# Row sums of the attention: an adding DMA puts the second key tile's probabilities into the first, and the probabilities are laid out by query tiles, then heads

## The chip, the cores and the metric

The kernel runs on one core of a Trainium2 chip: TensorE (PE, with a separate track for weight loads), VectorE (DVE), ScalarE (ACT), GpSimd (POOL), SyncE (SP, which here only issues DMAs), an SBUF of 128 partitions, eight PSUM banks and 16 DMA engines. The metric is the device time of one execution in microseconds (us).

## What is computed

One transformer layer on x of 4 x 512 rows of 1024: causal attention with 32 query heads and 8 key/value heads of 32, residual and layer norm, then a gated feed-forward with ternary weights, residual and layer norm.

```python
q = _apply_rope(q, cos, sin); k = _apply_rope(k, cos, sin)
k = jnp.repeat(k, N_REP, axis=2); v = jnp.repeat(v, N_REP, axis=2)
scores = jnp.einsum('bqhd,bkhd->bhqk', q, k) / np.float32(np.sqrt(HEAD_DIM))
scores = scores + mask
attn = jax.nn.softmax(scores, axis=-1)
out = jnp.einsum('bhqk,bkhd->bqhd', attn, v).reshape(bsz, seq_len, -1) @ wo
x = _layernorm(x + out)
x = _layernorm(x + (silu(x @ gate_w.T) * (x @ up_w.T)) @ down_w.T)
```

## The kernel before

**Stages.** The first 70 us load and project, the attention lasts until about 735 us, the feed-forward takes the rest. The attention runs over 16 units (u: a batch and eight query heads), each of two groups (G: four query heads that share one key/value head). That makes 32 groups, q = 2u + G; this text counts them from one, so the 15th group is u = 7, G = 0.

**A group.** Its 512 keys are four tiles of 128, taken in the order j = 3, 2, 1, 0. Key tile j is seen only by the queries from 128 j on, so its probabilities are a tile `p32[j]` of 128 keys (partitions) by four heads by 512 - 128 j queries, in f32. For each tile PE makes scores by keys (`score_k`, L984), ACT takes the exponential into `p32[j]` (`exp`, L1139), POOL zeroes the causal triangle of the diagonal block (`causal`, a select, L1443), and PE multiplies with v (`pv`, L998) into bank 7, all four tiles accumulating.

**Row sums.** The sum over keys of each query is a product with a matrix of ones (`sums`, L1013) into bank 2. So that it need not run over four tiles, POOL adds tiles first (`presum`, L1451): tile 3 into the fitting columns of tile 2 after the product of tile 2, then tile 2 into tile 1 after the product of tile 1. The sum runs over two tiles, 512 and 384 columns; in the very last group, where nothing is presummed, over four. DVE then transposes the sums, takes reciprocals, transposes back and scales bank 7 (`sum_turn`, `att_scale`, L1291 to L1301). Only when this is done may the next group's first product write bank 7. The scaled rows are split into two f16 parts (`att_hi`, `att_lo`) and stored; the output projections of a batch (`proj out`, on L948 with `wo_parts`) read them back when all eight groups of that batch are stored.

**Reuse.** There is one set of `p32`. The exponential of a group's tile j waits for what last read that tile in the group before: its product, and the sum (tiles 0 and 1) or a presum (tiles 2 and 3).

**Other work in the same stage.** PE also runs the projections of later units (`proj q`, 24 matmuls of 256 columns per tile; `proj kv` and `proj out`, 512 columns), and scores by queries (`score_q`, L960, with a mask product L963) two units ahead, whose row maxima DVE takes (`row_max`, L1267). They are the filler between the dependent steps above.

**What sets the order.** A planner (`Plan`) gives every piece of work an engine, a rank, a duration, the pieces it must follow and a time until its result is seen elsewhere. It plays these through and writes down one fixed order per engine. The programs then issue their instructions in that order, each with its semaphore waits. An engine that waits holds up all that stands behind it.

## Time and profile before

| | us |
|---|---|
| median of 2 runs | 1869.38 (1867.28 to 1871.48) |
| the profiled execution's own time | 1868.12 |
| its span, first to last instruction | 1866.4 |
| PE busy | 1807.0 (97%) |
| DVE busy | 1187.7 (64%) |
| ACT busy | 710.5 (38%) |
| POOL busy | 543.6 (29%) |

Busy time is what the instructions of an engine cover, so overlapping matmuls count once. An engine's idle time is named after what ended it (its releaser). A row of the trace's timeline merges instructions that follow each other on one line, and its duration runs to the modelled end of the last one; matmuls overlap, so the time that a piece takes on PE is read from its start to the start of the next row.

### The profile page before, as it was taken

What the parts mean: (1) busy time and instruction counts of PE and PEld (TensorE: products, weight loads), DVE (VectorE), ACT (ScalarE), POOL (GpSimd) and SP (SyncE); (2) the same over time, 40 slices, a digit from 0 to 9 for tenths busy, and PEclk for the clock granted to TensorE, in tenths of its full rate; (3) what the DMA queues carried; (4) which work ended last, traced back from release to release, by engine and by line L of the source; (5) the groups of instructions that cost most, each with busy time, mean ns of one, the idle gap of its engine ahead of it and who ended that gap; (6) DMA issues with size and microseconds to landing.
All of it is one profiled execution on the core that took longest, in us unless ns stands there. A gap on an engine that the chain in (4) does not pass through costs nothing.

```text
span 1866.4 us, 27364 instructions
## 1 busy us (share of the span) xinstructions
PE 1807.0 (97%) x10528; PEld 882.0 (47%) x10528; DVE 1187.7 (64%) x2047; ACT 710.5 (38%) x1112; POOL 543.6 (29%) x845
## 2 busy tenths in 40 slices
PE   7889999999999998999999999999999999999997
PEld 4545655555555543444444444444444444444443
DVE  7877778668768764445544444745656765667645
ACT  5443444444434444436433343342232322222221
POOL 1354546456546564131000000211321211112103
PEclk9999999999999999999999999999999999999999
DMA  8543234334334398557644353649321211232301
GB/s 246 118 103 78 54 85 125 83 80 116 90 52 114 81 212 221 209 208 263 236 171 150 107 195 126 215 148 211 127 66 53 79 66 51 72 104 85 107 12 79
DMA packets 228162, 233.13 MB, mean 125 GB/s; under 512 B 183872, under 2 KB 184128, under 8 KB 228032
## 3 DMA queue, kind: packets, MB, share of 16 engines
q1 hardware_dynamic: 227168, 230.99, 42.2%
q8 instruction: 83, 1.36, 0.3%
q10 hardware_dynamic: 864, 0.39, 0.1%
q14 instruction: 47, 0.39, 0.1%
HBM read 122.55 MB, written 72.88 MB: 105 GB/s over the span
## 4 chain that ended last, share of the span: by engine, by line
PE 85%; DVE 6%; issue 3%; SPq 2%; POOL 2%; ACT 1%; DMA 1%; ACTq 0%; DVEq 0%; POOLq 0%
PE bank L1053 31%; PE bank L948 20%; PE bank L1074 13%; PE bank L1087 6%; PE bank L998 4%; PE bank L960 3%; PE bank L984 3%; PE bank L1013 2%; SPq L1587 2%; DVE down_forms L1391 1%; PE bank L963 1%; DVE gate_blocks L1385 1%; POOL p_tiles L1451 1%; DVE row_max L1267 0%; DVE up_blocks L1375 0%
## 5 line engine op out<-in xcount | busy, mean ns | idle before, releaser
L1053 PE MATMUL bank<-x_forms,weight_forms 128*128 128x512 f16 x3136 | 700.9, 379 | 12.7 <-DVE gate_blocks L1375 4.4
L1053 PEld LDWEIGHTS bank<-x_forms,weight_forms 128*128 128x128 f16 x3136 | 305.3, 98 | 387.0 <-DVE gate_blocks L1375 7.1
L1139 ACT ACTIVATE p_tiles<-bank 128x512 f32<-128x512 f32 (+1 forms) x352 | 193.0, 556 | 276.6 <-PE bank L984 273.5
L1267 DVE TENSOR_REDUCE row_max<-bank 128x1 f32<-128x384 f32 (+3 forms) x352 | 220.0, 636 | 98.2 <-PE bank L963 96.6
L1074 PE MATMUL bank<-down_forms 128*128 128x512 f16 x1152 | 259.6, 381 | 2.4 <-issue 2.4
L948 PE MATMUL bank<-wq_parts,xT_parts 128*128 128x256 f16 x1536 | 219.4, 275 | 8.9 <-DVE wq_parts L1231 8.7
L1410 DVE TENSOR_TENSOR acc<-bank,acc 128x512 f32<-128x512 f32 x188 | 127.6, 687 | 124.2 <-PE bank L1074 64.7
L1443 POOL TENSOR_SCALAR_AFFINE_SELECT p_tiles<-p_tiles 128x128 f32<-128x128 f32 (+2 forms) x352 | 139.0, 403 | 212.2 <-ACT p_tiles L1139 210.9
L1074 PEld LDWEIGHTS bank<-down_forms 128*128 128x128 f16 x1152 | 113.0, 98 | 139.7 <-issue 4.9
L948 PEld LDWEIGHTS bank<-wq_parts,xT_parts 128*128 128x128 f16 x1536 | 144.1, 98 | 56.8 <-issue 14.2
L948 PE MATMUL bank<-wo_parts,att_parts 128*128 128x512 f16 x672 | 170.1, 382 | 0.6 <-DMA att_parts<-att_spill 0.6
L1475 POOL TENSOR_TENSOR acc<-acc,down_forms 128x1024 f32<-128x1024 f32 x16 | 38.8, 2427 | 377.4 <-DVE acc L1410 377.4
L1087 PE MATMUL bank<-down_forms 128*128 128x512 f16 x560 | 133.6, 379 | 1.7 <-DVE down_forms L1391 1.7
L960 PE MATMUL bank<-k_stack,q_stack 96*128 96x512 f16 (+3 forms) x512 | 127.0, 303 | 5.1 <-DVE row_max L1267 5.1
L984 PE MATMUL bank<-q_stack,k_stack 98*128 98x384 f16 (+3 forms) x512 | 126.4, 301 | 4.6 <-ACT p_tiles L1139 3.1
L1451 POOL TENSOR_TENSOR p_tiles<-p_tiles 128x512 f32<-128x512 f32 (+1 forms) x62 | 115.8, 1868 | 49.4 <-PE bank L998 41.3
L1375 DVE TENSOR_TENSOR up_blocks<-bank,up_blocks 128x512 f32<-128x512 f32 x84 | 57.9, 690 | 112.9 <-PE bank L1053 59.6
L1214 ACT ACTIVATE down_forms<-gate_blocks 128x512 f16<-128x512 f32 x102 | 64.0, 628 | 136.4 <-DVE gate_blocks L1385 130.4
L998 PE MATMUL bank<-p_tiles,v 128*32 128x128 f32 (+3 forms) x1024 | 95.4, 453 | 11.6 <-POOL p_tiles L1443 10.4
L1375 DVE TENSOR_TENSOR gate_blocks<-bank,gate_blocks 128x512 f32<-128x512 f32 x84 | 57.8, 688 | 74.8 <-PE bank L1053 65.0
L948 PE MATMUL bank<-wkv_parts,xT_parts 128*128 128x512 f16 x384 | 98.3, 379 | 1.3 <-DVE wkv_parts L1231 1.3
L1458 POOL TENSOR_SCALAR rstd<-rstd 128x1 f32<-128x1 f32 x96 | 34.8, 363 | 220.2 <-DVE rstd L1329 213.8
(114 smaller groups left out, 1999.9 us busy)
## 6 DMA issues: line engine op xcount, KB each, us to landing
weight_forms_spill<-weight_forms SPq DMA_DIRECT2D x28, 896.0 KB, 5.7
weight_forms<-weight_forms_spill SPq DMA_DIRECT2D x28, 896.0 KB, 4.5
x_forms_spill<-x_parts SPq DMA_DIRECT2D x56, 256.0 KB, 2.4
w_page<-gateT SPq DMA_DIRECT2D x28, 512.0 KB, 5.0
w_page<-upT SPq DMA_DIRECT2D x28, 512.0 KB, 4.0
w_page<-downT SPq DMA_DIRECT2D x28, 512.0 KB, 4.3
att_spill<-att_made SPq DMA_DIRECT2D x64, 128.0 KB, 2.1
down_forms<-x_spill SPq DMA_DIRECT2D x16, 512.0 KB, 3.4
```

Of the source, the lines that this page charges most:

```text
L948: t = nc.tensor.matmul(dst, left[:, a, k, rows], right[:, c, k, cols], start=k == 0 and m == 0, stop=last)
L960: nc.tensor.matmul(to[:, h, :], qT[0:STK, u % QS, h0 + h, i * P:n], kT[0:STK, b % 2, kv_of(u, h0 + h), 0:n], start=h == 0, stop=False, ski ...
L984: t = nc.tensor.matmul(to[:, h, :], kT[0:STKM, b % 2, (u % UNITS) * UG + G, lo:lo + P], qT[0:STKM, u % QS, G * REP + h0 + h, lo:S], start= ...
L998: t = nc.tensor.matmul(bank[PV_BANK[q]][h * HD:(h + 1) * HD, lo:S], value, p32[j][:, h, :], start=j == NT - 1, stop=j == 0, tile_position= ...
L1053: t = nc.tensor.matmul(strassen[bank_set(use)][to][:, :], w_form[:, use % 4, A_FORMS[a_form], k * P:(k + 1) * P], xF[:, :, B_FORMS[b_form] ...
L1074: t = nc.tensor.matmul(to[:, :], hid_p[place_of(r)][:, k, a, i // 2 * P:(i // 2 + 1) * P], wd_p[place_of(r)][:, c, cols], start=r == round ...
L1087: t = nc.tensor.matmul(to[:, :], hid_f[r % NF % 3][:, HID_FORMS.index(a_form), a, pair * P:(pair + 1) * P], wd_f[r % NF % 3][:, DOWN_B[b_f ...
L1139: nc.scalar.activation(p32[j][:, h0:h0 + heads, :], bank[5 + m % 2][:, 0:heads * n].rearrange("p (h c) -> p h c", c=n), ACT.Exp, scale=SCO ...
L1267: nc.vector.tensor_reduce(mx[:, u % 2, i, h0:h0 + ROW_HEADS[i]], bank[3 + m % 2][:, 0:ROW_HEADS[i] * n].rearrange("p (h c) -> p h c", c=n) ...
L1410: nc.vector.tensor_tensor(dst, got[:, :], dst, ALU.add).then_inc(s_acc, 1)
L1443: nc.gpsimd.affine_select(out=block, in_=block, compare_op=ALU.is_ge, fill=0.0, base=0, pattern=[[0, KEY_HEADS[j]], [1, P]], channel_multi ...
L1451: nc.gpsimd.tensor_tensor(to, to, p32[j + 1][:, :, :], ALU.add).then_inc(s_pre, 1)
```

## The change

For the first 29 groups (`EARLY`) a DMA that adds, issued by POOL, puts `p32[1]` (which by then holds tiles 1 to 3) into the columns of `p32[0]` from 128 on, 768 KB, and the row sum runs over `p32[0]` alone. The last three groups are summed as before. So that both sides of the DMA are one run of 1536 numbers in each partition, `p32[j]` is laid out by query tiles, then heads, then queries in a tile, where it was heads, then queries. The sum waits for the DMA; the exponential of the next group's tile 1 waits for the DMA where it waited for the sum. The planner takes the DMA's issue at 1.2 us and its landing at 5.0 us and ranks these sums 3.5 us later; it then writes another order for the whole attention.

```diff
+EARLY = NU * UG - 3
+FOLD_ISSUE, FOLD_LANDS = 1.2, 5.0
+
+def summed(q):
+    return 1 if q < EARLY else 2 if q < NU * UG - 1 else NT
...
-        freed = [("pv", *last, j), ("sums", *last) if j < 2 else ("presum", *last, j - 1)] if q else []
+        freed = [("pv", *last, j), ("sums", *last) if j < summed(q - 1) else ("presum", *last, j - 1) if j > 1 else ("fold", *last)] if q else []
...
-        put(PE, at + 3.5, 3.0 if final else 1.5, "sums", u, G, takes="T", after=[("causal", *one)] + [("presum", u, G, 1)] * (not final))
+        if q < EARLY:
+            put(PO, at + 3.5, FOLD_ISSUE, "fold", u, G, after=[("pv", u, G, 0), ("presum", u, G, 1)], lands=FOLD_LANDS)
+        put(PE, at + (7 if q < EARLY else 3.5), (.9, 1.6, 2.2, 2.5)[summed(q) - 1], "sums", u, G, takes="T", after=[("causal", *one)] + (
+            [("fold", u, G)] if q < EARLY else [("presum", u, G, 1)] if not final else []))
...
-        p32 = [p_all[:, p_starts[j]:p_starts[j + 1]].rearrange("p (h c) -> p h c", h=REP) for j in range(NT)]
+        p32 = [p_all[:, p_starts[j]:p_starts[j + 1]].rearrange("p (i h c) -> p i h c", h=REP, c=P) for j in range(NT)]
...
-                        t = nc.tensor.matmul(bank[PV_BANK[q]][h * HD:(h + 1) * HD, lo:S], value, p32[j][:, h, :],
+                        t = nc.tensor.matmul(bank[PV_BANK[q]][h * HD:(h + 1) * HD, lo:S], value, p32[j][:, :, h, :],
...
-                    tiles = 2
-                    if u * UG + G == NU * UG - 1:
-                        tiles = NT
-                    else:
-                        on.wait_ge(s_pre, 2 * (u * UG + G + 1))
+                    q = u * UG + G
+                    tiles = summed(q)
+                    if tiles == 1:
+                        on.wait_ge(s_fold, 16 * (q + 1))
+                    elif tiles == 2:
+                        on.wait_ge(s_pre, 2 * (q + 1))
...
-                    nc.scalar.activation(p32[j][:, h0:h0 + heads, :], bank[5 + m % 2][:, 0:heads * n].rearrange(
-                        "p (h c) -> p h c", c=n), ACT.Exp, scale=SCORE_DOWN).then_inc(s_exp, 1)
+                    nc.scalar.activation(p32[j][:, :, h0:h0 + heads, :], bank[5 + m % 2][:, 0:heads * n].rearrange(
+                        "p (h i c) -> p i h c", h=heads, c=P), ACT.Exp, scale=SCORE_DOWN).then_inc(s_exp, 1)
...
-                    block = p32[j][:, h0:h0 + KEY_HEADS[j], 0:P]
+                    block = p32[j][:, 0, h0:h0 + KEY_HEADS[j], :]
...
-                    to = p32[j][:, :, P:S - j * P]
-                    nc.gpsimd.tensor_tensor(to, to, p32[j + 1][:, :, :], ALU.add).then_inc(s_pre, 1)
+                    to, more = (t.rearrange("p i h c -> p (i h c)") for t in (p32[j][:, 1:NT - j, :, :], p32[j + 1][:, :, :, :]))
+                    nc.gpsimd.tensor_tensor(to, to, more, ALU.add).then_inc(s_pre, 1)
+                elif kind == "fold":
+                    u, G = which
+                    q = u * UG + G
+                    on.wait_ge(s_pv, NT * (q + 1))
+                    on.wait_ge(s_pre, 2 * (q + 1))
+                    to, more = (t.rearrange("p i h c -> p (i h c)") for t in (p32[0][:, 1:NT, :, :], p32[1][:, :, :, :]))
+                    e.dma_start(to, more, accum_op=ALU.add).then_inc(s_fold, 16)
```

**Place one: PE at the end of the 15th group.** In the rows below `p_tiles,v` is a product with v, `p_tiles,ones` the row sum, `k_stack,q_stack` and `cmask,idB` a score by queries with its mask, `q_stack,k_stack` a score by keys, `wo_parts` and `wq_parts` projections. Before, from the group's last product on:

```order
L998 MATMUL bank<-p_tiles,v 32x512 x4
L1013 MATMUL bank<-p_tiles,ones 32x512 x4
L1013 MATMUL bank<-p_tiles,ones 32x384 x4
L948 MATMUL bank<-wo_parts,att_parts 128x512 x3
L984 MATMUL bank<-q_stack,k_stack 128x256 x2
L960 MATMUL bank<-k_stack,q_stack 128x512
L963 MATMUL bank<-cmask,idB 128x128
L948 MATMUL bank<-wo_parts,att_parts 128x512 x3
L984 MATMUL bank<-q_stack,k_stack 128x256 x2
L948 MATMUL bank<-wo_parts,att_parts 128x512 x3
L998 MATMUL bank<-p_tiles,v 32x128 x4
```

Now, from the same product on (line numbers are those of the changed kernel):

```order
L1013 MATMUL bank<-p_tiles,v 32x512 x4
L999 MATMUL bank<-q_stack,k_stack 128x256 x2
L975 MATMUL bank<-k_stack,q_stack 128x512
L978 MATMUL bank<-cmask,idB 128x128
L963 MATMUL bank<-wo_parts,att_parts 128x512 x3
L999 MATMUL bank<-q_stack,k_stack 128x256 x2
L963 MATMUL bank<-wo_parts,att_parts 128x512 x3
L975 MATMUL bank<-k_stack,q_stack 128x512
L978 MATMUL bank<-cmask,idB 128x128
L963 MATMUL bank<-wo_parts,att_parts 128x512 x3
L999 MATMUL bank<-q_stack,k_stack 128x384
```

and on to the sum:

```order
L975 MATMUL bank<-k_stack,q_stack 128x512
L978 MATMUL bank<-cmask,idB 128x128
L963 MATMUL bank<-wo_parts,att_parts 128x512 x3
L999 MATMUL bank<-q_stack,k_stack 128x384
L963 MATMUL bank<-wo_parts,att_parts 128x512 x3
L975 MATMUL bank<-k_stack,q_stack 128x512
L978 MATMUL bank<-cmask,idB 128x128
L963 MATMUL bank<-wo_parts,att_parts 128x512 x3
L975 MATMUL bank<-k_stack,q_stack 128x512
L978 MATMUL bank<-cmask,idB 128x128
L963 MATMUL bank<-wq_parts,xT_parts 128x256 x6
L1029 MATMUL bank<-p_tiles,ones 32x512 x4
```

The sum stood right behind the last product and ran over two tiles; now 21 rows of other work stand between, and it runs over one. The next group's first product (32x128), which stood nine rows behind the sum, now stands behind it further on, next to the second and third.

**Place two: POOL at the same time.** Selects (`AFFINE_SELECT`), presums (`p_tiles<-p_tiles` on L1451 before, L1469 now) and rope sums. Before, from the second presum of the 15th group on:

```order
L1451 TENSOR_TENSOR p_tiles<-p_tiles 128x4x256
L1443 AFFINE_SELECT p_tiles<-p_tiles 128x128 x3
L1443 AFFINE_SELECT p_tiles<-p_tiles 128x512
L1443 AFFINE_SELECT p_tiles<-p_tiles 128x2x128 x2
L1443 AFFINE_SELECT p_tiles<-p_tiles 128x128
L1451 TENSOR_TENSOR p_tiles<-p_tiles 128x4x128
L1443 AFFINE_SELECT p_tiles<-p_tiles 128x128 x3
```

Now, from the second presum of that group on:

```order
L1469 TENSOR_TENSOR p_tiles<-p_tiles 128x1024
L1461 AFFINE_SELECT p_tiles<-p_tiles 128x128 x3
L1461 AFFINE_SELECT p_tiles<-p_tiles 128x512
L1476 DMA p_tiles<-p_tiles 128x1536
L1461 AFFINE_SELECT p_tiles<-p_tiles 128x256 x2
L1461 AFFINE_SELECT p_tiles<-p_tiles 128x128 x5
```

The DMA stands behind the select of the next group's first tile, and the next group's first presum is no longer among these rows: it has moved behind eight small instructions of a layer norm, directly ahead of the second presum.

**Place three: PE between the eighth group's sum and the ninth group's last product.** The eighth group is the last of the first batch. Before, from the ninth group's first product on:

```order
L998 MATMUL bank<-p_tiles,v 32x128 x4
L998 MATMUL bank<-p_tiles,v 32x256 x4
L948 MATMUL bank<-wq_parts,xT_parts 128x256 x6
L984 MATMUL bank<-q_stack,k_stack 128x384
L948 MATMUL bank<-wq_parts,xT_parts 128x256 x3
L960 MATMUL bank<-k_stack,q_stack 128x384
L963 MATMUL bank<-cmask,idB 128x128
L948 MATMUL bank<-wq_parts,xT_parts 128x256 x6
L984 MATMUL bank<-q_stack,k_stack 128x384
L948 MATMUL bank<-wq_parts,xT_parts 128x256 x3
L960 MATMUL bank<-k_stack,q_stack 128x384
L963 MATMUL bank<-cmask,idB 128x128
```

Now, from the eighth group's sum on:

```order
L1029 MATMUL bank<-p_tiles,ones 32x512 x4
L999 MATMUL bank<-q_stack,k_stack 128x384 x2
L975 MATMUL bank<-k_stack,q_stack 128x256 x2
L978 MATMUL bank<-cmask,idB 128x2x128
L975 MATMUL bank<-k_stack,q_stack 128x256 x2
L978 MATMUL bank<-cmask,idB 128x2x128
L999 MATMUL bank<-q_stack,k_stack 128x512
L986 MATMUL bank<-idH,max_parts 16x128 x4
L999 MATMUL bank<-q_stack,k_stack 128x512 x2
L1013 MATMUL bank<-p_tiles,v 32x128 x4
L1013 MATMUL bank<-p_tiles,v 32x256 x4
L1013 MATMUL bank<-p_tiles,v 32x384 x4
```

The query projections (`wq_parts`) that stood among these rows are gone from here; they now stand earlier. Scores and the three products remain.

## Rows read from the trace of the kernel before

**Rows 1.** Stretches (us): length, busy (xcount) PE, PEld, DVE, ACT, POOL; PEclk, DMA share, GB/s

```profile
70.00:200.00 130.00, 120.34 (x965) 65.77 (x964) 95.88 (x190) 57.80 (x104) 64.91 (x101) 0.96 0.41 91
200.00:300.00 100.00, 97.66 (x801) 55.01 (x798) 77.19 (x147) 43.13 (x77) 51.26 (x87) 1.00 0.33 80
200.00:700.00 500.00, 495.10 (x3878) 271.46 (x3878) 372.30 (x719) 221.21 (x388) 272.05 (x447) 1.00 0.43 101
```

**Rows 2.** The chain that ended last, shares of the span by engine

```profile
PE 85%; DVE 6%; issue 3%; SPq 2%; POOL 2%; ACT 1%; DMA 1%; ACTq 0%; DVEq 0%; POOLq 0%
```

**Rows 3.** PE's waits, 200 to 700 us: us in total, times, longest

```profile
PE bank L960 <- DVE row_max L1267: 1.9, 3, 1.5
...
PE bank L998 <- POOL p_tiles L1443: 0.9, 2, 0.5
```

**Rows 4.** Instructions by line: shapes, xcount, busy us, mean ns, idle before

```profile
L1013 PE MATMUL bank<-p_tiles,ones 128*32 128x384 f32 (+3 forms) x528 | 55.6, 541 | 0.0
```

**Rows 5.** PE's timeline at 618 us: start us, duration us, line, operation, xcount

```profile
617.92 1.06 PE L998 MATMUL bank<-p_tiles,v 128*32 128x512 f32 x8
618.80 1.69 PE L1013 MATMUL bank<-p_tiles,ones 128*32 128x512 f32 x16
620.42 0.50 PE L948 MATMUL bank<-wq_parts,xT_parts 128*128 128x256 f16 x3
```

**Rows 6.** PE's timeline behind the 15th group's sum

```profile
382.12 1.69 PE L1013 MATMUL bank<-p_tiles,ones 128*32 128x512 f32 x16
383.74 0.82 PE L948 MATMUL bank<-wo_parts,att_parts 128*128 128x512 f16 x3
384.39 0.38 PE L984 MATMUL bank<-q_stack,k_stack 98*128 98x256 f16 x2
...
385.76 0.81 PE L948 MATMUL bank<-wo_parts,att_parts 128*128 128x512 f16 x3
386.50 0.43 PE L998 MATMUL bank<-p_tiles,v 128*32 128x128 f32 x8
386.86 0.39 PE L960 MATMUL bank<-k_stack,q_stack 96*128 96x512 f16 x1
...
388.97 0.64 PE L998 MATMUL bank<-p_tiles,v 128*32 128x256 f32 x8
389.54 0.34 PE L984 MATMUL bank<-q_stack,k_stack 98*128 98x384 f16 x1
...
391.29 0.33 PE L984 MATMUL bank<-q_stack,k_stack 98*128 98x384 f16 x1
391.46 0.38 PE L960 MATMUL bank<-k_stack,q_stack 96*128 96x512 f16 x1
...
392.39 0.33 PE L984 MATMUL bank<-q_stack,k_stack 98*128 98x384 f16 x1
```

**Rows 7.** DVE's timeline behind the same sum

```profile
383.87 0.72 DVE L1291 STREAM_TRANSPOSE over_sum<-bank 128x512 f32<-128x512 f32 x1 [1.67 <-PE bank L1013]
...
385.65 0.69 DVE L1301 TENSOR_TENSOR over_sum<-bank,over_sum 128x512 f32<-128x512 f32 x1
```

**Rows 8.** POOL by line and shape, 60 to 740 us, columns as in rows 4

```profile
L1443 POOL TENSOR_SCALAR_AFFINE_SELECT p_tiles<-p_tiles 128x128 f32<-128x128 f32 x256 | 87.5, 350 | 109.5 <-ACT p_tiles L1139 108.2
L1451 POOL TENSOR_TENSOR p_tiles<-p_tiles 128x1024 f32<-128x1024 f32 x31 | 74.0, 2386 | 12.1 <-PE bank L998 11.2
L1437 POOL TENSOR_TENSOR rope_cos<-rope_cos,rope_sin 128x256 f32<-128x256 f32 x70 | 58.7, 839 | 34.2 <-DVE rope_sin L1254 34.0
L1451 POOL TENSOR_TENSOR p_tiles<-p_tiles 128x512 f32<-128x512 f32 x31 | 41.9, 1350 | 37.3 <-PE bank L998 30.1 <-issue 7.2
```

**Rows 9.** The selects: ns min/median/max, first and last start, forms

```profile
L1443 POOL TENSOR_SCALAR_AFFINE_SELECT p_tiles<-p_tiles x352: 282/293/1626, 70.1 to 730.9; 128x128 f32<-128x128 f32 x128, 128x256 f32<-128x256 f32 x32, 128x512 f32<-128x512 f32 x16
```

**Rows 10.** DMA issues: xcount, KB each, median us from issue to landing

```profile
weight_forms<-weight_forms_spill SPq DMA_DIRECT2D x28, 896.0 KB, 4.5
...
down_forms<-x_spill SPq DMA_DIRECT2D x16, 512.0 KB, 3.4
...
x_spill<-row SPq DMA_DIRECT2D x14, 512.0 KB, 2.6
...
q_stack<-stack_rows SPq DMA_TRANSPOSE x64, 3.2
```

More of the change, by code:

```diff
@@ L729, in block_kernel @@
         s_sk, s_exp, s_caus, s_pv = sem("score_k"), sem("exp"), sem("causal"), sem("pv")
-        s_pre, s_sums = sem("presum"), sem("sums")
+        s_pre, s_fold, s_sums = sem("presum"), sem("fold_dma"), sem("sums")
         s_scale_att, s_ahi, s_alo = sem("att_scaled"), sem("att_hi"), sem("att_lo")
@@ L880, in attention_over @@
             on.wait_ge(s_pre, 2 * (NU * UG - 1))
+            on.wait_ge(s_fold, 16 * EARLY)
             on.wait_ge(s_sums, NU * UG)
@@ L1005, in tensor_program @@
                     trans_free((kind, *which))
-                    tiles = 2
-                    if u * UG + G == NU * UG - 1:
-                        tiles = NT
-                    else:
-                        on.wait_ge(s_pre, 2 * (u * UG + G + 1))
+                    q = u * UG + G
[4 more added lines that the diff above has]
+                        on.wait_ge(s_pre, 2 * (q + 1))
                     for j in range(tiles):
                         for h in range(REP):
-                            t = nc.tensor.matmul(bank[TRANS][h * HD:(h + 1) * HD, j * P:S], ones[:, :], p32[j][:, h, :],
+                            t = nc.tensor.matmul(bank[TRANS][h * HD:(h + 1) * HD, j * P:S], ones[:, :], p32[j][:, :, h, :],
                                                  start=j == 0, stop=j == tiles - 1, tile_position=(0, h * HD))
@@ L1134, in scalar_program @@
                     on.wait_ge(s_pv, q * NT - j)
-                    if j < 2:
+                    if j < summed(q - 1):
                         on.wait_ge(s_sums, q)
+                    elif j == 1:
+                        on.wait_ge(s_fold, 16 * q)
                     else:
                         on.wait_ge(s_pre, 2 * q - (j - 2))
-                    nc.scalar.activation(p32[j][:, h0:h0 + heads, :], bank[5 + m % 2][:, 0:heads * n].rearrange(
-                        "p (h c) -> p h c", c=n), ACT.Exp, scale=SCORE_DOWN).then_inc(s_exp, 1)
+                    nc.scalar.activation(p32[j][:, :, h0:h0 + heads, :], bank[5 + m % 2][:, 0:heads * n].rearrange(
+                        "p (h i c) -> p i h c", h=heads, c=P), ACT.Exp, scale=SCORE_DOWN).then_inc(s_exp, 1)
                 elif kind == "att_hi":
```

## The prediction

> **What bounds the kernel now.** I read the stages first: in the attention, from 200 to 700 us, TensorE (PE) is busy 495.1 of 500 us, VectorE (DVE) 372.3, ScalarE (ACT) 221.2, GpSimd (POOL) 272.1, at a granted clock of 1.00 [rows 1]. The chain that ended last is PE for 85% of its length [rows 2]. So time here is PE's list of work, run in a fixed order: what shortens the list shortens the stage, as long as no new wait appears. PE's largest waits in those 500 us are 1.9 us for row maxima; for POOL it is 0.9 [rows 3]. Ahead of 200 us PE idles 9.7 us in 130 [rows 1].
>
> **What is removed.** Line L1013 holds the row sums: 528 matmul records, 55.6 us busy [rows 4]. One group of four heads is seen whole from 618.80 to 620.42: both tiles, 1.62 us. The product with v just ahead, the same eight records over one tile of 512 columns, takes 617.92 to 618.80, 0.88 us [rows 5]. A sum over the first tile alone should cost that, so 0.74 us goes per group; 29 of the 32 groups are changed: 29 x 0.74 = 21.5 us, 1.2% of the run and the most that the change can give.
>
> **What is added on PE's path: the fold's latency F.** The sum now waits for the adding DMA (the fold), and that for the group's last product with v, its second presum, and POOL. F has three terms.
> - From PE to another engine: 0.13 us (the sums end at 383.74, VectorE starts at 383.87) [rows 6, 7].
> - The issue on POOL. No row shows a DMA issued there. POOL instructions on 128 partitions last from 0.29 us (the median select) to 2.39 (a presum) [rows 8, 9]; I take 1.0.
> - Issue to landing of 768 KB. No row shows an adding DMA. As one read and one write: 512 KB land in 3.4 us and 896 KB in 4.5, so 1.1 us per 384 KB and 4.1 us here. If the destination is read too, 1536 KB on the same line give 6.3; if read and write follow each other, 2 x 4.1 = 8.2. A source in SBUF may be quicker, since 512 KB out of SBUF land in 2.6, 0.8 less [rows 10]. I take 5.5, which is two reads less that 0.8, because a sum needs both operands.
>
> So F is 6.6, with ends 4.5 (0.13 + 0.29 + 4.1) and 10.7 (0.13 + 2.39 + 8.2).
>
> **Does PE have work for that time?** In the 15th group all rows between the last product and the sum are in the trace of before, from 383.74 to 392.39, 8.65 us. That stretch also holds four pieces that now stand elsewhere: an output piece (0.65), two products (0.36 with 0.09 of wait, and 0.57) and a score piece (0.17) [rows 6]. That leaves 6.8 us, just enough. Counting the other groups over the new order with the same price per kind of row, 26 of the 29 have 6.6 to 8.8 us (mean 7.4).
>
> After the sum comes a second stretch. The sum frees the bank: transpose, reciprocal, transpose, product on VectorE, 383.87 to 386.34, 2.5 us, and only then may the next group's first product go [rows 6, 7]. The three early products therefore stand together and late, and the presums behind them: 1.35 + 2.39 us on POOL, then select, rope sum and two selects (0.35, 0.84, 0.35, 0.35) [rows 8] before the next group's last product. From the sum's start: 0.9 for the sum, 2.5 + 0.2 for the bank, 1.0 for the first two products, 3.7 and 1.9: 10.2 us. With F and 0.9 for the last product itself a group needs 17.7 us from one last product to the next. Counting PE's rows of each such cycle, 23 of 29 have more. Short are the second (12.9 us), third (16.5), seventh (15.0), eighth (9.3) and 28th (16.6), and the 29th has 3.5 us ahead of its sum. In the eighth, the last of the first batch, the output projections need that very group's result, so nothing is left to run. These lose 4.8 + 1.2 + 2.7 + 8.4 + 1.1 + 3.1 = 21.3 us. Part is idle in the same places already: PE loses 9.7 us before 200 us, of which I let 3 cover the second and third, and 2.3 us between 200 and 300 [rows 1]. 16 us remain.
>
> In the other 23 groups there is about 1 us to spare, while POOL's rows are sometimes long (a select: median 0.29, maximum 1.63) [rows 9]. I allow 0.1 us each, 2 us.
>
> **What costs nothing.** The fold's issue holds POOL for 1.0 us; behind it stand the next group's second selects and rope sums, and the products that wait for these now come 10 us later. Without that cover it would be 29 us. The next group's exponentials over the second tile wait for the fold instead of the sum; the scores behind them stand after the sum on PE. The other layout leaves columns per matmul and elements per exponential, select and presum as they were; ACT is idle 56% and POOL 46% of the stage, and 0.1 us on each of 11 exponentials a group would lie inside that. Transfers: the DMA engines are 43% busy [rows 1], the stack transposes land in 3.2 us [rows 10], and the fold shares the engines with them; that stays in the bounds of F.
>
> Sum on the profiled execution's own 1868.1 us: - 21.5 + 16 + 2 = - 3.5, so 1864.6, said as 1865. The median of the runs shown, 1869.4, is 1.3 above that execution.
>
> **The rivals.** A later fold costs each of the six short cycles its full delay and the others what goes past their 6.6 to 8.8 us.
> 1. *Two full reads.* F = 0.13 + 1.0 + 6.3 = 7.5: 16 + 5 + 7 + 2 - 21.5 = + 8.5, 1877 us. For it: both operands must be fetched. Against: the rows behind 6.3 read HBM. The Trainium skill, Collectives: The Full Stack, section "The bandwidth ceiling: the fold count and why AG ≠ RS ≠ AR", says that an add inside a DMA engine runs at about half a copy's rate, because its two source reads share one ring. No run here shows that yet.
> 2. *Two reads beside the other transfers* (slower than before). F = 8.4 when loads and transposes stretch it by 0.9: 16 + 11 + 22 + 2 - 21.5 = + 29.5, 1898 us. Any F above 7.0 ends in a loss. For it: 43% busy engines; against: the landings above were under load too.
> 3. *Read and write in turn.* F = 9.4: 16 + 17 + 44 + 2 - 21.5 = + 57, 1925 us. No row excludes it.
> 4. *POOL becomes the path.* The presums behind the late products cost 0.75 us in each of 23 groups, 17 us instead of 2: 1880 us. For it: 1 us of cover; against: POOL is idle 46%.
> 5. *A stretched issue.* A select of 1.63 instead of 0.29 us lost 1.33; were each fold's issue hit so, F = 7.9: 16 + 8 + 13 + 2 - 21.5, 1886 us. Against: the mean 128-column select is 0.35 [rows 8], so few are hit. The Trainium skill, SBUF — State Buffer, section "SBUF: two separate sides", warns that GpSimd cannot write DMA descriptors while VectorE runs a two-port operation. The long selects would fit such a lock; no row shows a descriptor being written.
> 6. *No relief.* PE's shorter list is met by another wait (VectorE is 74% busy, and the row maxima pace the scores), so that nothing is won and the short cycles stay: 1868 + 16, 1884 us. Against: only 1.9 us of such waits now.
>
> **How the numbers follow.** Forecast 0.52 (own range 1854 at F = 4.5, where the short cycles cost 5, to 1868 at F = 7.0); rival 1 0.18, rival 2 0.10, rival 3 0.07, rival 4 0.06, rival 5 0.04, rival 6 0.03. The range 1850 to 1898 reaches to rival 2; it leaves out rival 3, the upper half of rival 2 and a few hundredths below, under 0.2. About 2%, 37 us, is what a measurement of this kernel can tell from no change. A gain of 37 is out of reach of a 21.5 us term: 0.01. A loss of 37 needs F near 8.7: rival 3 and a third of rival 2, 0.11. The rest, 0.88, is within 2%.
>
> **What would show it.** The sums: four heads over one tile in 0.9 us, some 33 us in all instead of 55.6. The fold's row: issue to landing 5 to 6 us. PE from 200 to 700 us: idle some 20 us, most of it between 200 and 250, and only small waits at the other sums. If each sum shows a wait, F was too small, and the excess times 29 is the loss. Over 10 us of products waiting on POOL's selects would be rival 4. The stage after the attention should only shift. Wrong altogether would be a landing above 8 us, or sums that did not shrink.

## The result and the profile after

The changed kernel takes 1924.1 us (median of two runs, 1919.0 and 1929.2) against 1869.4: 1.029 times as long, 95% interval 1.017 to 1.042. A second series, in the experiments, gave 1921.5 and a ratio of 1.0272 (1.0243 to 1.0301). The forecast was 1865, its range ended at 1898. The profiled execution took 1929.16 us with a span of 1927.3, 60.9 more than before.

The stretches after, columns as in [rows 1]:

```profile
70.00:200.00 130.00, 116.09 (x849) 63.15 (x850) 90.49 (x176) 53.60 (x97) 65.64 (x100) 0.89 0.56 117
...
200.00:700.00 500.00, 462.86 (x3525) 255.72 (x3526) 351.27 (x685) 204.45 (x368) 273.22 (x439) 0.97 0.57 118
700.00:800.00 100.00, 77.44 (x484) 29.72 (x485) 45.31 (x82) 37.36 (x66) 45.52 (x82) 0.91 0.96 200
```

The stretch before that [rows 1] lacks:

```profile
700.00:800.00 100.00, 93.78 (x502) 39.64 (x495) 45.66 (x83) 45.38 (x70) 34.59 (x64) 0.97 0.67 212
```

From 70 to 800 us PE now idles 13.9 + 37.1 + 22.6 = 73.6 us, where it idled 9.7 + 4.9 + 6.2 = 20.8: 53 more. The granted clock, 1.00 over the middle stage before, is 0.97, and 0.89 instead of 0.96 ahead of it. A stretch at clock c loses (1 - c) of its length if PE works all through it: 14 + 15 + 9 = 38 us against 5 + 0 + 3 = 8, so at most 30 more. At full clock the short sums give 19 back (below, in the run of short sums in the old order). 53 + 30 - 19 = 64 is a little above the 61 seen, as it must be, since a low clock costs nothing while PE idles.

PE's largest waits from 60 to 800 us (in all, times, longest), before:

```profile
PE bank L998 <- POOL p_tiles L1443: 10.4, 7, 3.6
PE bank L960 <- DVE row_max L1267: 5.1, 9, 1.5
```

and after:

```profile
PE bank L1029 <- DMA p_tiles<-p_tiles: 24.5, 10, 11.3
PE bank L975 <- DMA q_stack<-stack_rows: 17.6, 5, 10.0
PE bank L999 <- ACT p_tiles L1157: 10.2, 12, 3.9
PE bank L975 <- DVE row_max L1285: 8.6, 15, 1.9
```

The first row is the sums' wait for the fold. The second was not in the forecast: scores waiting for the transposes of the stacks, which PE's list of before does not have. The third is scores waiting for a bank that an exponential has yet to read. A second profile of the same kernel (the changed kernel again, in the experiments) has the first at 10.6 us and the second at 21.4, so the first is the less stable one.

The sums, as in [rows 4], and the fold's line (ns min/median/max of the issue; landings in us):

```profile
L1029 PE MATMUL bank<-p_tiles,ones 128*32 128x512 f32 (+3 forms) x296 | 41.1, 642 | 24.5 <-DMA p_tiles<-p_tiles 24.5
```

```profile
L1476 POOL DMA_DIRECT2D p_tiles<-p_tiles x29: 855/875/1053, 83.1 to 725.3; - x29
...
DMA to landing us min/median/max: 5.7/6.9/17.3
```

And the stack transposes; first their landings before, where [rows 10] had 3.2 us, then after:

```profile
DMA to landing us min/median/max: 3.0/3.1/6.5
```

```profile
L1557 SPq DMA_TRANSPOSE q_stack<-stack_rows x64: 1232/1274/9487, 18.0 to 708.9; - x64
...
DMA to landing us min/median/max: 3.0/3.9/14.3
```

One place shows how it goes wrong. At 332.5 us POOL issues a fold, and then SyncE (SP) a transpose, a page load, a store and the next transpose. The rows are SP's timeline, PE's, and four stretches there:

```profile
332.58 1.27 SPq L1557 DMA_TRANSPOSE q_stack<-stack_rows  x1
333.96 1.63 SPq L1546 DMA_DIRECT2D page<-xT  x1
336.67 0.34 SPq L1600 DMA_DIRECT2D x_forms_spill<-x_parts  x1
337.22 9.49 SPq L1557 DMA_TRANSPOSE q_stack<-stack_rows  x1
```

```profile
336.18 0.81 PE L963 MATMUL bank<-wkv_parts,xT_parts 128*128 128x512 f16 x3
346.97 0.50 PE L975 MATMUL bank<-k_stack,q_stack 96*128 96x384 f16 x1 [9.98 <-DMA q_stack<-stack_rows]
```

```profile
330.00:337.00 7.00, 6.18 (x44) 3.13 (x41) 5.86 (x12) 3.24 (x6) 6.80 (x9) 1.00 0.84 145
337.00:347.00 10.00, 0.03 (x1) 0.03 (x2) 0.19 (x1) 0.00 (x0) 2.36 (x3) 0.73 0.96 96
347.00:350.00 3.00, 3.00 (x11) 1.48 (x12) 1.27 (x3) 1.12 (x2) 0.29 (x1) 0.50 1.24 174
347.00:365.00 18.00, 18.00 (x113) 8.62 (x114) 14.15 (x25) 7.70 (x15) 9.35 (x12) 0.87 0.62 134
```

The DMA engines are 96% busy while they move 96 GB/s, less than in the 7 us ahead. This fold takes 15.7 us to land, the two transposes 14.3 and 13.6; PE goes on when the first of them has landed (332.58 + 14.3 = 346.9). PE, VectorE and ScalarE stand for 10 us, and then PE runs at a granted clock of 0.87 for 18 us (0.50, its lower level of 1.2 GHz, in the first three) while it is fully busy. In the second profile the same wait is 10.4 us long.

### The profile page after: what moved, and what is told of

It reads as the page before. It is cut to its first block, busy times and chain, and to the rows that moved or that the text cites. A ratio compares the mean times of both kernels' runs of the same rounds, so it can differ in the third digit from the quotient of the medians.

```text
span 1927.3 us, 26931 instructions
## 1 busy us (share of the span) xinstructions
PE 1813.2 (94%) x10296; PEld 879.1 (46%) x10296; DVE 1190.7 (62%) x2047; ACT 704.9 (37%) x1112; POOL 567.2 (29%) x874
## 4 chain that ended last, share of the span: by engine, by line
PE 73%; DMA 9%; DVE 7%; POOL 4%; issue 4%; SPq 2%; ACT 1%; ACTq 0%; DVEq 0%; POOLq 0%
PE bank L1069 30%; PE bank L963 14%; PE bank L1090 13%; PE bank L1103 6%; DMA p_tiles<-p_tiles 3%; PE bank L1013 3%; DMA q_stack<-stack_rows 3%; PE bank L999 3%; PE bank L975 2%; POOL p_tiles L1469 2%; DMA x_forms<-x_forms_spill 1%; DVE down_forms L1409 1%; PE bank L1029 1%; SPq L1612 1%; PE bank L978 1%
## 5 line engine op out<-in xcount | busy, mean ns | idle before, releaser
L1069 PEld LDWEIGHTS bank<-x_forms,weight_forms 128*128 128x128 f16 x3136 | 305.8, 98 | 391.6 <-issue 13.7
L1157 ACT ACTIVATE p_tiles<-bank 128x512 f32<-128x512 f32 (+1 forms) x352 | 187.6, 555 | 286.1 <-PE bank L999 160.5
L963 PE MATMUL bank<-wq_parts,xT_parts 128*128 128x256 f16 x1536 | 214.4, 277 | 8.8 <-DVE wq_parts L1249 8.7
L975 PE MATMUL bank<-k_stack,q_stack 96*128 96x512 f16 (+3 forms) x512 | 129.6, 311 | 27.2 <-DMA q_stack<-stack_rows 17.6
L999 PE MATMUL bank<-q_stack,k_stack 98*128 98x384 f16 (+3 forms) x512 | 126.6, 311 | 12.6 <-ACT p_tiles L1157 10.2
L1469 POOL TENSOR_TENSOR p_tiles<-p_tiles 128x512 f32<-128x512 f32 (+1 forms) x62 | 121.4, 1959 | 38.6 <-PE bank L1013 35.4
L963 PEld LDWEIGHTS bank<-wo_parts,att_parts 128*128 128x128 f16 x672 | 63.6, 99 | 73.7 <-issue 10.4
```

The lines of the kernel that those rows point to most:

```text
L963: t = nc.tensor.matmul(dst, left[:, a, k, rows], right[:, c, k, cols], start=k == 0 and m == 0, stop=last)
L975: nc.tensor.matmul(to[:, h, :], qT[0:STK, u % QS, h0 + h, i * P:n], kT[0:STK, b % 2, kv_of(u, h0 + h), 0:n], start=h == 0, stop=False, ski ...
L999: t = nc.tensor.matmul(to[:, h, :], kT[0:STKM, b % 2, (u % UNITS) * UG + G, lo:lo + P], qT[0:STKM, u % QS, G * REP + h0 + h, lo:S], start= ...
L1069: t = nc.tensor.matmul(strassen[bank_set(use)][to][:, :], w_form[:, use % 4, A_FORMS[a_form], k * P:(k + 1) * P], xF[:, :, B_FORMS[b_form] ...
L1157: nc.scalar.activation(p32[j][:, :, h0:h0 + heads, :], bank[5 + m % 2][:, 0:heads * n].rearrange("p (h i c) -> p i h c", h=heads, c=P), AC ...
L1469: nc.gpsimd.tensor_tensor(to, to, more, ALU.add).then_inc(s_pre, 1)
```

## Experiments

The differences are medians against the kernel before in the same series (1869.2 to 1871.3). Theory 1 puts the loss on the fold's latency, theory 2 on its load beside other transfers. Diffs are against the changed kernel unless another is named.

**The fold of 4 columns.**
```diff
-                    e.dma_start(to, more, accum_op=ALU.add).then_inc(s_fold, 16)
+                    e.dma_start(to[:, 0:4], more[:, 0:4], accum_op=ALU.add).then_inc(s_fold, 16)
```


> The changed kernel, its order kept, but the adding DMA carries 4 columns (2 KB over all partitions) instead of 1536, so the row sums of 29 groups lack most of the second key tile's part. Theory 1 (the landing of the full fold is longer than TensorE's work in reserve) and theory 2 (the full fold and the transposes of the stacks hold each other up) both expect that the loss goes and the shorter sums are won: landing near 2 to 3 us, time 1845 to 1858. The rival that the new order itself costs (three products standing late and together, presums behind them) expects 1880 or more although the DMA is small. If it comes out between, at 1860 to 1875, the order costs about what the shorter sums give.

1870.0 us, - 0.6, ratio 0.9995 (0.9982 to 1.0009). Landing 2.0/2.5/4.0 us. The loss is gone, but nothing is won, though the sums are short: the last branch, that the order costs about what the shorter sums give. Both theories missed that. So the loss needs the full transfer.

**The full fold, awaited by no sum.**
```diff
-                    if tiles == 1:
-                        on.wait_ge(s_fold, 16 * (q + 1))
...
+                            part = p32[0][:, 0:1, h, :].broadcast_to([P, NT, P]) if tiles == 1 else p32[j][:, :, h, :]
```


> The changed kernel, its order kept, with the full fold of 768 KB moved as before, but the row sums do not wait for it: they read the first 128 columns of the first tile four times, so 29 groups get other sums. The exponentials over the second tile still wait for the fold. Theory 1 (the loss is the sums' own wait for the landing, 24.5 us in 10 places, and what the clock makes of it) expects nearly the time of the small fold, within 8 us of it. Theory 2 (the fold delays the transposes and loads that scores wait for) expects the waits of the scores for the stacks to stay near 17 us, transposes up to 10 us and more in landing, and 15 to 45 us above the small fold.

1919.1 us, + 48.5, ratio 1.0267 (1.0232 to 1.0303): 49 above the small fold, 3.7 below the changed kernel, each taken against before in its series. The scores' waits for stacks stay, and those behind exponentials grow (60 to 800 us):

```profile
PE bank L999 <- ACT p_tiles L1156: 23.7, 21, 4.3
PE bank L975 <- DMA q_stack<-stack_rows: 15.0, 5, 8.2
```

So the sums' own wait is a small part, and theory 2 holds for the larger one, a little above its 45 us. But the next group's exponentials still wait for the fold in this run. PE's listed waits add up to 67.5 us, 36.6 with the small fold. Of the 31 more, 14 are the scores' waits for stacks, and some 5 end right behind an exponential that had waited for the fold. The 49 us are thus not load alone; no run has the full fold awaited by nobody.

**A plain copy of the same bytes.**
```diff
-                    e.dma_start(to, more, accum_op=ALU.add).then_inc(s_fold, 16)
+                    e.dma_start(more, to).then_inc(s_fold, 16)
```


> The changed kernel with a plain copying DMA of the same 768 KB between the same two places, from the first tile to the second, nothing added; the sums wait for it and lack the second tile's part. If the addition costs a second read (what I took when I set 5.5 us), the uncontended landing falls from 5.7 to 4.1 to 5.0 us and the time to 1880 to 1905. If size and path alone set it, the landings stay at 5.7 to 6.9 and the time at 1915 to 1930.

The copy goes from the first tile to the second, the other way round. 1880.0 us, + 9.4, ratio 1.0045 (1.0030 to 1.0060). Landing 3.5/4.4/6.6 us. The first branch holds at its lower end; the least landing is below its 4.1. The fold's queue on the page (packets, MB, share of 16 engines' span), first with the copy, then with the fold that no sum awaited:

```profile
q0 software_dynamic: 4176, 22.81, 3.2%
```

```profile
q0 software_dynamic: 4176, 22.81, 6.4%
```

Per fold that is 0.032 x 1878 / 29 = 2.1 us of all 16 engines for the copy and 0.064 x 1913 / 29 = 4.2 us for the addition. Stack transposes landed in at most 6.3 us beside the small fold, 7.4 beside the copy and 12.6 beside this addition.

**The fold on GpSimd itself.**
```diff
-FOLD_ISSUE, FOLD_LANDS = 1.2, 5.0
+FOLD_ISSUE, FOLD_LANDS = 3.6, .15
...
-                    e.dma_start(to, more, accum_op=ALU.add).then_inc(s_fold, 16)
+                    nc.gpsimd.tensor_tensor(to, to, more, ALU.add).then_inc(s_fold, 1)
```


> The changed kernel with the fold done by GpSimd itself, 1536 columns of addition instead of a DMA, and planned so (3.6 us, then at once there). By the presums (1024 columns in 2.39 us, 512 in 1.35) it takes 3.4 to 3.6 us, and the sum may start 3.8 us after the last product instead of 7.9. Theories 1 and 2 expect no long waits for the fold or the transposes and 1848 to 1862. The rival that GpSimd becomes the path (29 x 2.6 us more work on it) expects products waiting over 15 us in all for selects, and 1870 to 1890.

1892.2 us, + 21.7, ratio 1.0117 (1.0095 to 1.0140), above both branches. The fold takes 3.43 us as estimated; the planner's other durations make another order. Neither branch named what grew:

```profile
PE bank L975 <- DVE row_max L1285: 24.5, 23, 3.0
...
PE bank L1013 <- POOL p_tiles L1461: 5.1, 5, 2.1
```

The scores wait for VectorE's row maxima, not for selects. Over the whole program VectorE's 2047 instructions take 1234.9 us on the page, 1192.8 with the small fold. Most of the 42 us lies on one line, first with the small fold, then with GpSimd's (60 to 800 us):

```profile
L1279 DVE TENSOR_TENSOR stack_rows<-rope_cos,stack_rows 128x256 f16<-128x256 f32 x70 | 45.7, 653 | 21.5 <-ACT stack_rows L1142 21.0
```

```profile
L1279 DVE TENSOR_TENSOR stack_rows<-rope_cos,stack_rows 128x256 f16<-128x256 f32 x70 | 81.0, 1157 | 21.6 <-ACT stack_rows L1142 21.1
```

This line reads and writes SBUF alone; the row maxima, which read a bank of PSUM, take 636 and 635 ns in the mean. The row maxima behind it start later. The Trainium skill, SBUF — State Buffer, section "SBUF: two separate sides", says that GpSimd and a VectorE operation with two inputs in SBUF lock each other out of a shared pair of ports; these rows agree.

**The layout alone.**
```diff
-EARLY = NU * UG - 3
+EARLY = 0
```


> The other layout of the probabilities alone: no group is folded, all sums go over two tiles as before, the order is that of before. What I wrote (the layout is free) expects the time of before within 3 us, 1867 to 1873. If exponentials, selects or presums suffer from the layout, 5 us and more above it.

1867.8 us, - 2.1, ratio 0.9985 (0.9975 to 0.9994): the layout costs nothing.

**An order made for a later landing.**
```diff
-FOLD_ISSUE, FOLD_LANDS = 1.2, 5.0
+FOLD_ISSUE, FOLD_LANDS = 0.9, 7.0
```


> The changed kernel, with one figure of the planner changed: it counts 0.9 us for the fold's issue and 7.0 for its landing instead of 1.2 and 5.0, so the order leaves more work ahead of each sum. If the sums' own waits for the fold (24.5 us in 10 places) were the loss, most of them go and the time falls to 1895 to 1905. If the adding transfer's load on the DMA engines is the loss, as the run in which nobody's sum waited suggests (1919), the scores' waits for the stacks stay and the time is 1910 to 1930.

1901.9 us, + 32.1, ratio 1.0179 (1.0153 to 1.0205). The time lies in the first branch, and the sums wait only 2.4 us in all, as it says. But the scores' waits for stacks fall too, from the second profile's 21.4 us to 12.1, and transposes land in at most 9.8 us. So 20 us of the loss came from an order made for a landing of 5.0 us, and not through the sums alone.

**A small fold in an order made for it.**
```diff
-FOLD_ISSUE, FOLD_LANDS = 1.2, 5.0
+FOLD_ISSUE, FOLD_LANDS = 0.9, 1.5
...
-        put(PE, at + (7 if q < EARLY else 3.5), (.9, 1.6, 2.2, 2.5)[summed(q) - 1], "sums", u, G, takes="T", after=[("causal", *one)] + (
+        put(PE, at + (4.5 if q < EARLY else 3.5), (.9, 1.6, 2.2, 2.5)[summed(q) - 1], "sums", u, G, takes="T", after=[("causal", *one)] + (
```


> The fold of 4 columns again (most of the second tile's part is missing from 29 groups' sums), but the order is made for a fold that lands 1.5 us after an issue of 0.9 instead of 5.0 after 1.2, and the sums are due 2.5 us earlier. With the order of the changed kernel the small fold took 1870, no less than before although the sums are 21.5 us shorter. If the late place of the sums (and with it the early products, which wait for the bank) ate that gain, it comes back here: 1850 to 1860. If another engine paces the attention whatever the order, the time stays at 1866 to 1874.

1871.9 us, + 2.1, ratio 1.0012 (0.9999 to 1.0024), in the second branch. By the waits, 9.0 us in 10 places for the small fold took what the order might have won, so this run settles little.

**No fold in the six short groups.**
```diff
+FOLDS = [q for q in range(EARLY) if q not in (1, 2, 6, 7, 27, 28)]
...
-    return 1 if q < EARLY else 2 if q < NU * UG - 1 else NT
+    return 1 if q in FOLDS else 2 if q < NU * UG - 1 else NT
```


> The changed kernel without the fold in the six groups that I had counted as short of work (the second, third, seventh, eighth, 28th and 29th); these sum two tiles as before, 23 groups are folded. My own sum said that these six lose 16 us net and gain 4.4: it expects 12 us less than the changed kernel. If the adding transfers cost about the same per fold wherever they are (54 us over 29), 6 of them give back 8 to 14 us too; the waits tell the two apart: by my sum the waits at sums go in these places alone, by the other the scores' waits for transposes shrink. The 29th group's fold waited 11.3 us beside the loads of the next stage, so with that gone I expect 1895 to 1908.

1885.3 us, + 15.5, ratio 1.0078 (1.0063 to 1.0093): 37 below the changed kernel's second series (+ 52.2), three times the 12 us of my own sum and 10 us below the range that I expected. The waits:

```profile
PE bank L983 <- DMA q_stack<-stack_rows: 8.3, 3, 4.8
PE bank L1037 <- DMA p_tiles<-p_tiles: 6.9, 7, 1.7
```

Against the second profile of the changed kernel the scores' waits fall by 13.1 us, the sums' by 3.7, and the clock from 200 to 700 us is 1.00 instead of 0.96. The 10 us wait at 347 us is gone too, although the group there is still folded: the order shifted, and with it what the transfers meet.

**Smaller pieces.**
```diff
-                    to, more = (t.rearrange("p i h c -> p (i h c)") for t in (p32[0][:, 1:NT, :, :], p32[1][:, :, :, :]))
-                    e.dma_start(to, more, accum_op=ALU.add).then_inc(s_fold, 16)
+                    to, more = (t.rearrange("p i h c -> p (i h c)").rearrange("p (m n c) -> p m n c", m=2, n=2)
+                                for t in (p32[0][:, 1:NT, :, :], p32[1][:, :, :, :]))
+                    for n in range(2):
+                        e.dma_start(to[:, :, n, :], more[:, :, n, :], accum_op=ALU.add).then_inc(s_fold, 16)
```


> The changed kernel with each fold issued as two adding DMAs of half the columns each, interleaved, so that every piece is 1536 bytes long instead of 6144; the bytes and the work are the same, the issues on GpSimd twice as many (29 x 0.9 = 26 us more on it). The transposes landed in up to 14.3 us beside the full fold, 12.6 with nobody's sum waiting, 7.4 beside the plain copy and 6.3 beside the small fold. If long pieces stand ahead of the transposes' short ones in the engines, shorter pieces let them pass: landings of at most 8 us, and 1895 to 1910. If the engines' time for the addition is what counts, the landings stay above 9 and the time at 1912 to 1935.

1952.5 us, + 83.3, ratio 1.0460 (1.0417 to 1.0503), worse than either. Each half takes 1.38 us to issue and 6.2 to land, the queue's share is 7.9%, transposes land in at most 11.9 us, and the sums wait 45.3 us. Shorter pieces did not let the transposes pass. How much of the loss is issue time and how much load, this run doesn't tell apart.

**The small fold without the six groups.** The two edits together, of the small fold and of the six groups.

> The fold of 4 columns (most of the second tile's part is missing from the folded groups' sums) in 23 groups alone; the six that I had counted as short of work sum two tiles as before. The small fold in 29 groups took 1870. If what the sums save was eaten by those six groups, as my sum has it (16 us), it comes back: 23 x 0.74 = 17 us, less 2 for the rest: 1852 to 1858. If other engines pace the attention, so that nothing is won wherever PE's list is shorter, the time stays at 1866 to 1872.

1867.6 us, - 1.7, ratio 0.9994 (0.9980 to 1.0008). Leaving the six groups out won 37 us with the full fold and 1 with the small one: they are no sink of their own.

**Six groups less, and the later landing.** The two edits together.

> The full fold in 23 groups (not in the six short ones) with the order made for a landing of 7.0 us. Each alone took 1885 and 1902 against 1924. If they take away different losses (places without work, and orders that are too tight), the two together reach 1870 to 1880; if both had only moved the transposes out of the folds' way, nothing adds: 1883 to 1900.

1884.7 us, + 15.4, ratio 1.0077 (1.0048 to 1.0105), the same as without the second: what the later landing gave alone (20 us) lay within the 37 of the six groups.

**The changed kernel again.**

> The changed kernel itself once more, beside the others: 1915 to 1930, since its first two runs gave 1919 and 1929. It fixes the difference to the runs above.

1921.5 us, + 52.2.

**Short sums in the old order.** Against the layout alone, with the planner's durations of before:
```diff
-                    tiles = summed(q)
+                    tiles = 1 if q < NU * UG - 3 else summed(q)
```


> The kernel before in every engine's order and every wait, with the other layout (which cost nothing, 1868), and with one thing changed: the sums of the first 29 groups run over the first tile alone and so lack the second tile's part. It is the pure removal of 21.5 us from TensorE's list, with no fold and no new wait. If the list bounds the attention, as I read rows 1 to 3, it takes 1848 to 1852. If something else paces the attention, so that small folds in any order gave 1868 to 1872, it stays above 1862 and the trace shows whose waits grow.

1857.9 us, - 11.6, ratio 0.9936 (0.9915 to 0.9957): about half of 21.5, between the two expectations. The sums and the wait that grew most:

```profile
L1026 PE MATMUL bank<-p_tiles,ones 128*32 128x512 f32 (+3 forms) x296 | 36.5, 577 | 0.0
```

```profile
PE bank L1012 <- DVE over_sum L1316: 4.6, 4, 1.6
```

The records shrink by 55.6 - 36.5 = 19.1 us. Of this, 6 go to PE's other waits, 27.4 us from 60 to 800 instead of 21.4; most of it is the next group's product waiting for the bank, 4.6 us instead of 1.0. VectorE's 2.5 us behind each sum stay [rows 6, 7]; that PE has less to do beside them is my reading.

**The new order, no fold at all.**
```diff
-                    if tiles == 1:
-                        on.wait_ge(s_fold, 16 * (q + 1))
-                    elif tiles == 2:
+                    if tiles < NT:
...
-                    e.dma_start(to, more, accum_op=ALU.add).then_inc(s_fold, 16)
```


> The order of the changed kernel without any fold: the sums run over the first tile alone (the second tile's part is missing) as soon as the presums are done, and the next exponentials wait for the sums' input no longer than before. With a fold of 4 columns this order took 1870. If the small fold's own 3.5 us of latency cost that (exponentials over the second tile waited 13.5 us for it in 6 places), it falls to 1850 to 1856; if the order itself costs it, with its late sums and the early products bunched behind them, it stays at 1864 to 1871.

1869.5 us, 0.0, ratio 0.9995 (0.9980 to 1.0010), so the order itself costs 11.6 us. Its waits:

```profile
PE bank L998 <- ACT p_tiles L1154: 10.8, 8, 7.7
PE bank L974 <- DVE row_max L1282: 9.3, 15, 2.6
```

**The fold beside the old order.** Against the layout alone:
```diff
+        if q < NU * UG - 3:
+            put(PO, at + 3.5, FOLD_ISSUE, "fold", u, G, after=[("pv", u, G, 0), ("presum", u, G, 1)], lands=FOLD_LANDS)
...
+                            part = p32[0][:, 0:1, h, :].broadcast_to([P, NT, P]) if tiles == 1 else p32[j][:, :, h, :]
```


> Close to the order of before, two-tile sums' places kept, with the full fold of 768 KB issued in 29 groups; the sums do not wait for it and read the first 128 columns of the first tile four times (so other sums). The exponentials over the second tile wait for the fold. If the adding transfers cost some 49 us wherever they are, as between the small fold and the fold that no sum awaited, this takes 1895 to 1920. If only the changed order brought folds and transposes together, it takes under 1880.

1881.9 us, + 12.4, ratio 1.0063 (1.0043 to 1.0084): 24 above the short sums alone, half of the 49 in the new order, just above the second expectation. Little of it is load on others: PE's listed waits grow from 27.4 to 45.2 us, the scores' waits for stacks by 4.0 of that (5.5 from 1.5), while 13.7 end right behind an exponential that had waited for the fold. In this order the fold's own latency shows there; that load costs much in any order is not shown.

```profile
PE bank L999 <- ACT p_tiles L1158: 20.9, 16, 3.6
...
PE bank L975 <- DMA q_stack<-stack_rows: 5.5, 4, 2.9
```

**The fold on VectorE, in 29, 23 and 22 groups.** The diff is that of the 23 groups. The planner takes the fold at 1.8 us and ranks the sums 2 us earlier than in the changed kernel (2.5 in the last run), so the orders differ too.
```diff
+                    nc.vector.tensor_tensor(to, to, more, ALU.add).then_inc(s_fold, 1)
...
-        if q < EARLY:
-            put(PO, at + 3.5, FOLD_ISSUE, "fold", u, G, after=[("pv", u, G, 0), ("presum", u, G, 1)], lands=FOLD_LANDS)
+        if q in FOLDS:
+            put(VE, at + 3.5, FOLD_ISSUE, "fold", u, G, after=[("pv", u, G, 0), ("presum", u, G, 1)])
```


> The changed kernel with the fold done by VectorE itself (1536 columns, 1.7 us estimated from its busy time per column in the other rows; planned as 1.8), correct in all its parts. It moves nothing on the DMA engines and lands 2 us after the last product. If the transfers were the loss, 1862 to 1872 like the small fold. If VectorE, 74% busy, then paces the scores by its row maxima (29 x 1.7 = 49 us more work), 1880 to 1900, with waits of the scores for row maxima above 20 us as in the fold by GpSimd (24.5 us).

> The fold by VectorE in 23 groups, the six short ones sum two tiles as before; correct in all its parts. In 29 groups it took 1873, with two single waits of 7.2 and 5.4 us near the first groups and the last ones. If those came from folds in the short groups, it takes 1858 to 1866; if VectorE's 40 us of more work eat whatever is won, 1867 to 1875.

> The same without the fold in the first group too (22 folds), its sums due half a microsecond earlier and the planner's durations of the two-tile sums as before the change. 1856 to 1866 if the first groups are the sore place, 1867 to 1875 if VectorE's work is.

Time: 1873.2 us (+ 3.7; ratio 1.0019, 1.0004 to 1.0034), 1858.1 (- 13.3; 0.9932, 0.9913 to 0.9952) and 1859.4 (- 11.9; 0.9944, 0.9923 to 0.9964). The fold takes 1.76 us. With 23 folds the middle stage is whole again although VectorE is busier:

```profile
200.00:700.00 500.00, 491.68 (x3769) 266.29 (x3768) 411.57 (x750) 224.29 (x396) 290.62 (x460) 1.00 0.43 105
```

This computes the same sums as the changed kernel and takes 0.7% less than before, 3.3% less than the change (0.9932 / 1.0272).

## Why the prediction was wrong

The runs give the sum again, in the forecast's terms: short sums - 11.6, the new order + 11.6, a small fold in it about 0, the full fold in place of the small one + 49, the sums' waiting for it + 3.7: + 52.

**Transfers, the step that failed.** "What costs nothing" counted the fold's transfers at nothing, from a mean of 43% busy engines and transposes of 3.2 us, with the words "that stays in the bounds of F". With the full fold in the place of a small one the same order takes 49 us more, before any sum waits. F prices only those who wait for the fold. The larger part was paid by others: the stack transposes, which land in up to 14.3 us where it was 6.5 at most, and the scores behind them (17.6 us of waits in one profile, 21.4 in the other, none in the list of before). How the 49 us divide between these, the exponentials that wait for the fold, and the clock is read from waits, not measured by a run. And a mean of 43% hides the fuller places, such as the 67% from 700 to 800 us before the change, which became 96%.

**F.** The issue was right (0.88 us against 1.0). The landing was too small by 1.4 us, 6.9 against 5.5; its least, 5.7, is what I took for the usual one. F is 0.13 + 0.88 + 6.9 = 7.9. By my own working (rival 5 stood at 7.9) that would have been 1886. An order planned for a landing of 7.0 does give 20 us back. But the sums' waits are not the 36 us over that account: in the second profile they are 10.6.

**What is removed.** 0.74 us per group was nearly right in records (19.1 us of 21.5; the sums take 36.5 in all where I wrote 33, and 41.1 in the changed kernel at its lower clock), but worth 11.6 at the end: 6 of the missing 7.5 us are other waits of PE. The sentence that time here is PE's list "as long as no new wait appears" hid this: such waits appear even with no fold, most of them for the bank that VectorE's chain behind the sum frees.

**Short cycles.** I gave the six 16 us net for waits at and behind their sums. Leaving them out won 37 with the full fold, 1 with a small one, and the waits that went were at transposes more than at sums. The new order, on the other hand, costs 11.6 with no fold at all, and my sum had no term for that: PE waits 10.8 us for exponentials and 9.3 for row maxima in it.

**The clock** was left out. Behind the 10 us stop PE's granted clock was 0.87 for 18 us, where it had been 1.00 ahead of it; over 70 to 800 us that is at most 30 of the 61 us.

**The rivals.** Rival 3 named 1925, the right number for a wrong reason: it needs F = 9.4. Rival 2 had half the cause: the landings do stretch beside other transfers, but the price lay with those. Rival 1's double reading holds: addition takes twice the engines' time of a copy (6.4% against 3.2%). The Trainium skill, Collectives: The Full Stack, section "The bandwidth ceiling: the fold count and why AG ≠ RS ≠ AR", says of a ring of cores that its adding step runs at half the rate of its copying step, because the add needs two source reads; the trace agrees in engine time, less so in landing (6.9 against 4.4 us). Rival 4 did not come: products wait 7.0 us in all for selects. Nor did rival 5: no issue took more than 1.05 us. The warning of the Trainium skill, SBUF — State Buffer, section "SBUF: two separate sides", thus does not show in these 29 rows. Rival 6 was true of the new order: shorter sums and no gain.

Open is why the addition costs five times what the copy does (49 against 10 us, waits of exponentials and sums included in the copy's) for twice the engine time; the rows only show engines 96% busy at the long stops, moving little.

## What to carry to other kernels

A transfer put into a kernel is priced twice: by how long its own user waits, and by what it does to the transfers in flight beside it; for the second, look at the DMA share where others' landings are already waited for, not at the mean. Work taken off the longest engine is worth less than its length where a chain over other engines starts at its end: leave it out in the unchanged order first, since that run shows what its removal is worth before anything is put in its place (here 11.6 us; the best run, with the fold on VectorE, gave 13.3). The step of 1536 columns was cheaper here on an engine with 26% to spare than as a transfer whose latency a new order must hide.

## What the runs showed of the hardware

- An adding transfer of 768 KB within SBUF, issued by GpSimd: issue 0.88 us, landing 5.7 us at the least, 6.9 in the median, 17.3 at most. The plain copy: 0.57, 3.5, 4.4 and 6.6.
- The same addition costs 1.76 us on VectorE and 3.43 on GpSimd. In the run with GpSimd's, a VectorE instruction from SBUF to SBUF took 1157 ns in the mean of 70, 653 in the run with the small fold; one from PSUM took the same in both.
- Cut into pieces of 1536 bytes instead of 6144, the same bytes took about a quarter more engine time (7.9% of 1947 us against 6.4% of 1921), and GpSimd issued for 2 x 1.38 us instead of 0.88.
- SP's issue of a transpose, 1.27 us in the median, took 9.49 in the stop at 337 us, with the engines 96% busy, and SP issued nothing else meanwhile. The plain copy occupied the engines for 2.1 us a time, the addition for 4.2.
